# One of four context sequences of a cross-attention tile transposed on chip from the copy that is loaded already

## The reference

```python
def _L0_xattn_ref(k, v, q, Wk, Wv, bv, Wq, bq, Wo, bo):
    kp = jnp.einsum('bsd,ed->bse', k, Wk)
    vp = jnp.einsum('bsd,ed->bse', v, Wv) + bv
    qp = jnp.einsum('bsd,ed->bse', q, Wq) + bq
    scores = jnp.einsum('bqd,bkd->bqk', qp, kp) * scale
    probs = jax.nn.softmax(scores, axis=-1)
    ctx = jnp.einsum('bqk,bkd->bqd', probs, vp)
    return jnp.einsum('bqd,ed->bqe', ctx, Wo) + bo
...
x = x + _L0_xattn_ref(ctx_1024, ctx_1024, _layernorm(x), Wk, Wv, bv, Wq, bq, Wo, bo)
x = x + _L0_attn_ref(_layernorm(x), ...)
x = x + _L0_ffn_ref(_layernorm(x), ...)
```

## Time and profile before

| | us |
|---|---|
| median of 3 runs | 910.84 |
| lowest and highest | 908.56, 913.74 |
| the profiled execution | 905.29 |
| its span, first to last instruction | 903.4 |

### The profile page before, as it was taken

One profiled execution on the slowest core, in us unless ns is written; L12 is line 12 of the kernel. 1 busy time (PEld: TensorE's weight loads), 2 busy tenths in 40 slices (PEclk: granted clock), 3 DMA queues, 4 the chain that ended last, 5 costly groups with the idle time before them and its releaser, 6 DMA issues.

```text
span 903.4 us, 24127 instructions
## 1 busy us (share of the span) xinstructions
PE 811.7 (90%) x9192; PEld 704.3 (78%) x9192; DVE 632.5 (70%) x973; ACT 540.0 (60%) x846; POOL 231.6 (26%) x133
## 2 busy tenths in 40 slices
PE   3889869999999999998582699999999999999994
PEld 2555539889999899896582579888898898888984
DVE  3234332647567475563648399999999999999992
ACT  2433326726445365352131188898999989999881
POOL 1344410000000000000000024554555545555541
PEclk9899999999999999998655599999999999999997
DMA  9799970000000000006372125454554554545542
GB/s 351 274 391 387 382 298 1 3 4 1 3 2 3 4 3 3 3 3 274 112 269 93 58 91 142 122 153 131 139 149 120 153 136 131 152 124 149 142 117 58
DMA packets 34663, 115.84 MB, mean 128 GB/s; under 512 B 4290, under 2 KB 15491, under 8 KB 29475
## 3 DMA queue, kind: packets, MB, share of 16 engines
q1 hardware_dynamic: 27010, 104.35, 33.3%
q0 software_dynamic: 7584, 10.49, 6.5%
HBM read 105.26 MB, written 9.57 MB: 127 GB/s over the span
## 4 chain that ended last, share of the span: by engine, by line
PE 82%; DMA 7%; DVE 6%; issue 2%; ACT 1%; SPq 1%; POOLq 0%; DVEq 0%; ACTq 0%
PE ps L428 21%; PE ps L429 20%; PE ps L430 20%; DMA ctx_t<-in_ctxT 4%; PE ps L734 3%; PE ps L614 3%; PE ps L593 2%; PE ps L602 2%; PE ps L686 2%; PE ps L507 1%; PE ps L671 1%; PE ps L485 1%; PE ps L664 1%; PE ps L697 1%; PE ps L504 1%
## 5 line engine op out<-in xcount | busy, mean ns | idle before, releaser
L403 POOL DMA_INDIRECT xs_sb<-xn_d,slot_row x39 | 68.4, 1753 | 461.6 <-DVE slot_row L1315 384.7
L1195 DVE TENSOR_TENSOR w_lo<-w,w_hi 128x1024 fp32r<-128x1024 f32 x156 | 185.3, 1207 | 0.4 <-issue 0.4
L910 ACT ACTIVATE w_hi<-w 128x1024 fp32r x156 | 161.4, 1064 | 8.4 <-DVE tile_e L1276 7.3
L414 POOL DMA_INDIRECT out_x<-y_sb,slot_row x39 | 120.2, 3082 | 123.0 <-ACT y_sb L942 123.0
L428 PE MATMUL ps<-w_hi,xh 128*128 128x512 f32 x312 | 127.2, 408 | 1.3 <-DVE xl L1338 1.3
L430 PE MATMUL ps<-w_hi,xl 128*128 128x512 f32 x312 | 122.9, 394 | 0.0
L429 PE MATMUL ps<-w_lo,xh 128*128 128x512 f32 x312 | 122.9, 394 | 0.0
L428 PE MATMUL ps<-xT_hi,wa_hi 128*128 128x256 f32 x384 | 112.6, 293 | 1.5 <-DVE xT_lo L1089 1.5
L429 PE MATMUL ps<-xT_lo,wa_hi 128*128 128x256 f32 x384 | 108.9, 284 | 0.0
L430 PE MATMUL ps<-xT_hi,wa_lo 128*128 128x256 f32 x384 | 108.7, 283 | 0.0
L921 ACT ACTIVATE w_hi<-w_sb 128x1024 fp32r<-128x1024 f32 x78 | 82.8, 1062 | 34.1 <-DMA w_sb<-in_w 29.7
(11 more groups left out here) (180 smaller groups left out, 1690.3 us busy)
## 6 DMA issues: line engine op xcount, KB each, us to landing
w_sb<-in_w SPq DMA_DIRECT2D x78, 512.0 KB, 4.7
ctx_t<-in_ctxT SPq DMA_DIRECT2D x16, 1028.0 KB, 7.6
ctx_n<-in_ctxN SPq DMA_DIRECT2D x16, 1024.0 KB
w<-in_w SPq DMA_DIRECT2D x8, 2048.0 KB, 12.0
stage<-in_w_a SPq DMA_DIRECT2D x16, 256.0 KB, 5.4
x_all<-in_x SPq DMA_DIRECT2D x4, 512.0 KB, 7.4
out_x<-x_all SPq DMA_DIRECT2D x1, 2048.0 KB, 13.8
xn_d<-xn SPq DMA_DIRECT2D x4, 512.0 KB, 4.4
```

The costliest lines, as they stand in the source:

```text
L403: pool.indirect_dma_start(xs_sb[:, :], None, xn_d, bass.IndirectOffsetOnAxis(slot_row[:, t:t + 1], 0)).then_inc(f_xs, 16)
L414: pool.indirect_dma_start(out, bass.IndirectOffsetOnAxis(slot_row[:, t:t + 1], 0), y_sb[:, :], None, compute_op=ALU.add).then_inc(f_st, 16)
L910: act.activation(w_hi[:, c, :].rearrange("p (c n) -> p c n", c=DC), w13[:, bass.ds(e, 1), c % 2, :, c // 2 * 512:(c // 2 + 1) * 512].rearr ...
L1195: dve.tensor_tensor(w_lo[:, c, :].rearrange("p (c n) -> p c n", c=DC), w13[:, bass.ds(e, 1), c % 2, :, c // 2 * 512:(c // 2 + 1) * 512].re ...
```

## The change

For the fourth sequence of each tile the tokens-on-partitions copy is no longer loaded. `ctx_n` is loaded for three sequences (768 KB where it was 1024 KB), and the fourth quarter is made on chip:

- PE, right behind `scores(t)`, transposes the four 128x128 blocks of `ctx_t` of sequence 3 into bank 6 (`ctx_tr`);
- ACT, first in its step, copies that bank (128x512) into `ctx_n` (`ctx_ev`).

Two semaphores come with it: `x_tn` (the transposes of a tile are done) and `x_cn` (the copy is done). The load of `ctx_t` now waits for `x_tn` in place of `x_sc`; `pv` waits for `x_cn` too. Since bank 6 is taken whole, `c_tr` moves to the free half of bank 2, beside the output of `tr`, and `tr` and `c_tr` get a wait each on the ACT copy of the other (`x_cT`, `x_xnT`), which stands earlier in ACT's order.

```diff
 def load(t, p):
-            wait(sp, x_sc, t - 1)
+            wait(sp, x_tn, t - 1)
             sp.dma_start(ctx_t...)
             wait(sp, x_pv, t - 1)
-            sp.dma_start(ctx_n[:, p, :, :, :]..., a["ctxN"][t, :, :]).then_inc(l_ctxN[p], 16)
+            sp.dma_start(ctx_n[:, p, 0:BT - 1, :, :]..., a["ctxN"][t, :, :]).then_inc(l_ctxN[p], 16)
...
 def tr(t, p):                         # PE
             wait(pe, x_xnT, t)
+            wait(pe, x_cT, t - 3)
...
+        def ctx_tr(t, p):
+            if not valid(t, NT):
+                return
+            wait(pe, x_cn, t)
+            for kc in range(KC):
+                for dc in range(DC):
+                    m = pe.transpose(ps[:, 6, (kc * DC + dc) * P:(kc * DC + dc + 1) * P],
+                                     ctx_t[:, p, BT - 1, dc, kc * P:(kc + 1) * P], ident)
+            m.then_inc(x_tn, 1)
...
 def pv(t, p):
             pe.wait_ge(l_ctxN[p], 16 * (t - p) + 32)
+            wait(pe, x_cn, t + 1)
...
 def c_tr(t, p):
             wait(pe, x_cT, t)
+            wait(pe, x_xnT, min(t + 4, NT) if isinstance(t, int) else t + 4)
             for dc in range(DC):
-                m = pe.transpose(ps[:, 6, dc * P:(dc + 1) * P], ...)
+                m = pe.transpose(ps[:, 2, D + dc * P:D + (dc + 1) * P], ...)
...
 def xstep(t, p):                      # PE
             scores(t, p)
+            ctx_tr(t, p)
             tr(t + 2, p)
...
 def cT_ev(t, p):                      # ACT
-            act.activation(cT[:, :, :], ps[:, 6, 0:D]...)
+            act.activation(cT[:, :, :], ps[:, 2, D:2 * D]...)
...
+        def ctx_ev(t, p):
+            if not valid(t, NT):
+                return
+            wait(act, x_tn, t + 1)
+            wait(act, x_pv, t - 1)
+            act.activation(ctx_n[:, p, BT - 1, :, :], ps[:, 6, :]..., ACT.Copy).then_inc(x_cn, 1)

 def xstep(t, p):                      # ACT
+            ctx_ev(t, p)
             xT_ev(t + 2, p)
```

10 lines of the change are left out of this document (6 added, 4 removed).

## The result

| | median us | range of the runs | profiled execution |
|---|---|---|---|
| before | 908.25 | 904.16 to 915.36, 22 runs | 905.29, span 903.4 |
| changed | 912.97 | 908.25 to 917.33, 22 runs | 915.56, span 913.7 |

The ratio is 1.0042, 95% interval 1.0022 to 1.0062. A second measurement of the same file gave 1.0058 (1.0030 to 1.0087). So the change costs 4 to 5 us, where -0.7 was forecast. The amount is inside the range given (903.8 to 915.5), but it is measurable, and it has the other sign.

A forecast was written before the change was run, and what follows sets the result against it. Loads were taken to bound the steady stretch at 6.28 us a step, with PE close; afterwards PE, at 6.08. Terms -2.3 + 1.0 + 0.0 + 0.6 = -0.7 us took 910.84 to 910.1 us, range 903.8 to 915.5.

The forecast's parts named there:

- just in time, at no cost: Steady steps, tile 3 to 15: `ctx_t` lands before its use 8.7 us after issue; the stretch gets 2.3 us shorter.
- The gated attention and the experts are untouched: Behind the cross-attention: no term in the sum, and the clock before them falls in the same idle stretch.
- rival four: Steady loads: landing time, not bytes, sets the step, which stays 6.28 us; only the ends count, +1.6, 912.4 us; chance 0.06.
- PE's work: Steady steps on PE: four transposes at 0.11 us add 0.44 us to 5.64, making 6.08 us a step.
- The rivals with 0.185 or 0.273 for each: Dearer transposes on PE: 0.185 us each gives 914.3 us, chance 0.10; 0.273 us each gives 919.2 us, chance 0.12.
- The base: Steady steps: PE's own work without waits for `ctx_t` or the layer norm, 5.64 us a step before the change.
- The signs named for this case: Steady stretch: PE still waiting for `ctx_t`, with the DMA share under 1 while the step stays 6.28 us.
- ACT's copy, DVE's layer norm, `ctx_n`, `ctx_l`, the new waits: Steady steps: 0.59 us copy, exp at 2.75 us, hidden by 0.8 us cover; layer norm wait goes; new waits cost nothing.
- The ends: Outside the steady stretch: start 1.0 us later, tile 1 to 3 unchanged at 0.0, end 0.6 us later.
- the exponential's wait for ACT: Last tile: exp waits for the bank's copy until about 2.4 us after the scores, 0.6 us later than before.
- rival two: Transposes on PE cost 0.185 us each, a step is 6.38 us, tile 1 to 3 adds 0.6; 914.3 us; chance 0.10.
- rival one: Steady loads are slower in timed runs than in the profile, so the median falls by 6.0 to 904.9 us; chance 0.20.

The follow-up runs named there:

- e7: Changed kernel with `ctx_t` asked for first, DVE's layer norm ahead of the residual sum, ACT's copy behind exp; timed once, 911.17 us... 911.16 us (before 914.35).
- e8: Kernel before with `ctx_t` asked for first and DVE's layer norm early, all of `ctx_n` loaded; timed once at 893.84 us (before 914.35).
- e10: e8's kernel again, timed with more runs: 897.57 us against 906.99 for the kernel before, ratio 0.9872.
- e12: e10 with 40 tiny unread transposes added on PE: 901.70 us against 906.99 for the kernel before, ratio 0.9933.
- e1: Changed kernel with SP asking for the next tile's `ctx_t` ahead of this tile's `ctx_n`; timed once at 911.17 us (before 905.11).
- e6: Changed kernel with SP asking for the next `ctx_t` ahead of `stage`, still behind `pv` and `ctx_n`; timed once at 912.96 us (before 914.35).
- e3: Kernel before with three quarters of `ctx_n` loaded, no transposes or copy, PE's work kept; timed once at 903.34 us (before 905.11).
- e5: Changed kernel with ACT's copy of the transposed context behind exp; timed once at 909.83 us (before 914.35).
- e9: Kernel before with 40 tiny unread transposes added on PE where it waits anyway: 914.78 us against 906.99, ratio 1.0093.
- e2: Kernel before with SP asking for the next tile's `ctx_t` ahead of this tile's `ctx_n`; timed once at 903.39 us (before 905.11).
- e15: Kernel before with only DVE's layer norm moved ahead of the residual sum, loads in old order; tile 3 to 15 took 81.12 us in its trace.
- e4: Changed kernel with all of `ctx_n` loaded and the on-chip copy put in an unread buffer; timed once at 911.40 us (before 905.11).
- e11: e7's kernel again, timed with more runs: 908.25 us against 906.99 for the kernel before, ratio 1.0000.
- e14: Changed kernel again, unedited, measured beside e13: 913.29 us against 907.28 for the kernel before, ratio 1.0058.
- e13: Changed kernel with two more PE steps in the loop instead of written out, plus 28 tiny transposes: 907.30 us against 907.28 before, ratio 0.9994.
- e17: Changed kernel with 87 small unread transposes added on PE: 910.51 us against 908.18 for the kernel before, ratio 1.0012.

## Why the prediction was wrong, point by point

Two steps failed. The first is the wait for the loads: "just in time, at no cost", which was to win 2.3 us, while PE went on waiting (5.9 us where 6.9 had been). The second is a term put at nothing, "The gated attention and the experts are untouched": its products are the same, but they took 4.8 us more on average over the traces. By the timed runs the second makes the loss. It is luck that 912.97 lies inside the range and beside rival four's 912.4. Rival four has the waits right, but it adds only the two ends to them, not the gated attention.

**PE's work.** Right. Four transposes cost 0.44 us a step (5.94 against 5.50, e7 and e8), and took 0.50 from their start to that of the next group. The rivals with 0.185 or 0.273 for each are out. The Trainium skill (TensorE: Matmul & The Clock Gate, Part 4: PE-mode transpose) gives about 275 ns, for bf16; for the float32 transposes here the trace has nearly that as the length of a record (287), not as the price of one in a row. The base was a little high: PE alone needs 5.50 a step (e8, e10, e12), not 5.64, which held other small gaps. A step of 5.94 plus what waits remain gave 6.52, 6.24 and 6.40 in three traces, against 6.08.

**The loads.** This step failed: "with 12% less to move and less queued, and 2 x 6.1 - 3.5 = 8.7 us until it is used, I take it as just in time, at no cost". I had the 9.6 us of the slowest round trip beside the 8.7 and argued it away with the bytes. (256 of 2312 KB are 11%, not 12%, but that changes nothing.) The way from `pv` to the landing is four requests one behind another and 7 us of a single transfer, and neither gets shorter by a ninth: 9.1 us on average in the changed kernel, 9.2 in the kernel before, against 8.3 that PE leaves. A busy share of 1.00 told nothing of a limit: the engines then moved 417 GB/s in e8. A change of the order of the requests (e1, e6) took the wait away; less to load (e3) made the stretch 0.6 us shorter. The signs named for this case did come: PE still waited for `ctx_t`, with the DMA share at 0.91. It is rival four, which had 0.06.

**ACT's copy, DVE's layer norm, `ctx_n`, `ctx_l`, the new waits.** As forecast: ACT's copy took 0.60 us, and the exponential started 2.5 us behind the scores (2.75 said) in the step from 57.52 on. There was no wait of PE for any of them, and none for `p_last` in the steps.

**The ends.** The start was 0.92 us longer (1.0 said), but by PE's own transposes at the lower clock: ACT's place, to which I gave it, changes nothing (e5). From tile 1 to 3 it was +0.4, +0.2 and +0.7 in three traces (0.0 said; 0.6 with rival two's price). The end was 1.05 us longer (0.6 said) in the changed kernel and in e5, and the traces split it in two. From tile 15's scores to PE's last projection it was 9.35 us where it had been 8.76: 0.59 us, and in all the other kernels with the change it was 9.34 or 9.35 too, with the copy first or late. So this part had the size that was said, but it is not the exponential's wait for ACT. The other 0.46 us come behind it: the four transposes of line 550 (565 in the changed kernel) ran at the lower clock, 0.47 us a record instead of 0.33. That happened in some traces of kernels without the change as well (e3, e8, e10, e12) and not in others, so it is no cost of the change. Without transposes the first part was 9.3 us in e8 and 10.0 in e9 too; I don't know what sets it there.

**The gated attention, "untouched".** This is the term that the sum lacked. 40 records more move the code against the grid. In six traces of kernels with the place of before (before, e2, e3, e8, e10, e15) it took 314.0 to 317.8 us, 315.9 on average; in eight with the change's 40 (changed, e1, e4, e5, e6, e7, e11, e14) 317.8 to 324.9, 320.7 on average: 4.8 us. 3.0 of them are the stops themselves, which sum to 6.4 and 9.4 us on average. With the code put elsewhere (e13, e17) the change cost -0.5 us (-2.9 to +1.9) and +1.1 us (-1.1 to +3.3), with e17's pads in it. So by the times nearly all of the 4 to 5 us comes from there, and the edit itself, in its own order of loads, costs about nothing. That is near the -0.7 forecast for it, but not by the forecast's terms: in no trace with that order did the stretch from tile 3 to 15 come out 2.3 us under 75.33 (74.86 to 78.25), and where no wait hides PE's work the transposes cost 6.5 us (e11 against e12). How much the place costs is less sure than that it does: e9's 40 records cost 7.8 us, more than the change with the same 40.

**What stays open.** The profiled executions show more than the times: the cross-attention is 2 to 5 us longer in four traces with the change (changed, e13, e14, e17), and the timed runs of e13 and e17 show at most 1. Traces of kernels without the change vary too: with the loads in its own order the cross-attention took 107.9 to 108.4 us in three traces (before, e3, e9) and 115.1 in e15. The profiled execution of the kernel before (905.29) was 3 us under its median, and that of the changed kernel (915.56) 2.6 above its own, so these two exaggerate, but by which stretch I can't tell, as timed runs leave no rows. The 5.55 us between median and profile on which rival one rested came from 3 runs; with 22 they are 3.0. And which points of the grid stop was not forecast, only that the same code stops when it is moved by a whole step: some packets start under 1 us after the last point of the grid, others over 4 us, and I don't know what sets that. That the packets carry PE's program is inferred from their number and their places; the profile does not name an engine for them.

## What to carry to other kernels

Before you credit a smaller load, follow one buffer round: from the event that frees it, through the requests ahead of it on the queue, to its landing and its use. If that is longer than the work that covers it, the order of the requests is the lever and the bytes are not; a DMA share of 1.00 does not decide it. When one wait is removed, price the one right behind it (here 0.7 us became 6.2), and remove both: that was worth 9 to 12 us, where the change itself lost. And where a change adds instructions to an engine whose program is long, compare its "issue" stops far behind the edit with the instruction packets, and time a padded control, before a difference of half a per cent is put down to the idea.

## What the runs showed of the hardware

- In the gated attention 46 instruction packets of 16,384 bytes went with 5884 matmul records, 127.2 a packet. PE stopped for 0.3 to 3.3 us at places on that grid, in all the traces, and went on 1.2 to 1.6 us after the end of the packet beside the stop. The profile calls this "issue". Behind some of the stops PE ran at the lower clock (granted 0.50 from 279.4 to 281.9), behind others not (1.00 from 167.0 to 169.5). Forty records of nothing ahead of that code cost 7.8 us (ratio 1.0093).
- DVE's tensor-scalar operation of 128x256 took 0.41 us alone and 0.53 to 0.98 where it overlapped POOL's operations by 0.3 us or more (e1).
- The DMA engines were busy for the whole stretch at 386 GB/s and, with requests made earlier, moved 417 GB/s.
- Four 128x128 transposes in a row took 0.50 us from start to start at the full clock, and 0.91 at the lower one; at the full clock each had a record of 0.29 us.
- A transpose of 4x4 costs 0.067 us in a group of 20, and 0.08 to 0.09 in groups of 43 to 67.
